# Three or four units per image sampled by matrix products beside an LSTM, in a four-stage image kernel on one core

## What is computed

```python
x = x + window_attention(gn(x))     # 8x8 query blocks, 14x14 keys, 4 heads of 8 channels
x = x + lstm(gn(x))                 # a sequence of 96 columns per image row, hidden size 128
x = x + deformable_conv(gn(x))      # 3x3, learned offsets and masks
x = x + block_transform(gn(x))      # M * block * M^T on 8x8 blocks
```

```python
x_off = g_lt * x[qx_lt, qy_lt] + g_rb * x[qx_rb, qy_rb] + g_lb * x[qx_lt, qy_rb] + g_rt * x[qx_rb, qy_lt]
x_off = x_off * m
out = conv2d(x_off, conv_w, stride=3)
```

## Time and profile before

| | us |
|---|---|
| median of 3 executions | 3617.43 |
| lowest, highest | 3611.35, 3619.76 |
| the profiled execution, its own time | 3624.01 |
| span of the profile, first to last instruction | 3622.2 |
| PE, DVE, POOL, ACT busy | 2785.3, 2479.2, 2380.0, 1263.4 |

### The profile page before, as it was taken

How to read it: one execution, slowest core, us unless ns; L and a number is a source line. 1 busy time by engine, 2 the same in 40 slices (tenths; PEclk the granted TensorE clock), 3 DMA queues, 4 the chain that set the end, 5 groups by cost and what they waited for, 6 DMA issues and landing times. The chain is left out here.

```text
span 3622.2 us, 59607 instructions
## 1 busy us (share of the span) xinstructions
PE 2785.3 (77%) x21833; PEld 2027.9 (56%) x21833; DVE 2479.2 (68%) x5480; ACT 1263.4 (35%) x3105; POOL 2380.0 (66%) x2445
## 2 busy tenths in 40 slices
PE   6979984885899748867998568668987376889882
PEld 4667763664676526646666346546665254555542
DVE  4754447985777669965777679756777675677763
ACT  4644433542433315523333145324333121222210
POOL 3200026777777777777777777777777777777774
PEclk9999996886899868876999779768999688999995
DMA  6622025764321346636212376543213432222211
GB/s 214 194 60 73 1 71 166 208 174 93 88 60 53 106 145 192 193 82 123 59 53 68 96 216 193 145 94 87 59 54 104 87 94 73 65 63 70 59 53 48
DMA packets 270803, 374.53 MB, mean 103 GB/s; under 512 B 109508, under 2 KB 181336, under 8 KB 269992
## 3 DMA queue, kind: packets, MB, share of 16 engines
q1 hardware_dynamic: 166688, 200.21, 19.2%
q0 software_dynamic: 76896, 157.64, 16.0%
q10 hardware_dynamic: 26928, 12.87, 1.6%
HBM read 270.08 MB, written 99.55 MB: 102 GB/s over the span
## 5 line engine op out<-in xcount | busy, mean ns | idle before, releaser
L769 POOL DMA_INDIRECT got<-sample_table,index x2403 | 2325.2, 968 | 1092.3 <-issue 726.6
L1618 PE MATMUL gates<-cells,row_hat 128*128 128x400 f32 x1782 | 653.3, 513 | 67.8 <-DVE spanned L1153 53.2
L1618 PEld LDWEIGHTS gates<-cells,row_hat 128*128 128x128 f32 x1782 | 332.7, 194 | 309.6 <-issue 84.2
L1175 DVE TENSOR_TENSOR got<-got,bank 128x864 f32<-128x864 f32 x267 | 279.6, 1047 | 242.5 <-DMA got<-sample_table,index 234.3
L852 ACT ACTIVATE pt<-gates 98x512 f32<-98x512 f32 x528 | 288.6, 594 | 325.8 <-PE gates L1726 304.7
L1826 PEld LDWEIGHTS gates<-hist,whh 128*128 128x128 f32 x2280 | 313.5, 205 | 138.7 <-DVE hist L1469 100.8
L1826 PE MATMUL gates<-hist,whh 128*128 128x96 f32 x2280 | 325.9, 290 | 53.8 <-DVE hist L1469 53.1
L1286 DVE TENSOR_REDUCE mx<-gates 128x2 f32<-128x392 f32 x576 | 295.5, 553 | 82.3 <-PE gates L1712 80.9
L1606 PE MATMUL bank<-turned,wout 128*128 128x96 f32 x1728 | 244.9, 304 | 131.5 <-DVE turned L1203 66.1
L1606 PEld LDWEIGHTS bank<-turned,wout 128*128 128x128 f32 x1728 | 239.0, 219 | 156.4 <-DVE turned L1203 110.5
L1712 PE MATMUL gates<-kst,qst 96*128 96x196 bf16 x1152 | 185.2, 278 | 119.7 <-DVE mx L1286 103.1
(11 more groups left out here) (188 smaller groups left out, 4791.6 us busy)
## 6 DMA issues: line engine op xcount, KB each, us to landing
kst<-k_parts SPq DMA_DIRECT2D x96, 441.0 KB
got<-sample_table,index POOLq DMA_INDIRECT x2403
qst<-q_parts SPq DMA_DIRECT2D x96, 288.0 KB
k_parts<-kp SPq DMA_DIRECT2D x24, 882.0 KB
k_parts<-kp SPq DMA_DIRECT2D x24, 588.0 KB
q_parts<-qp SPq DMA_DIRECT2D x24, 576.0 KB
spread<-locations ACTq DMA_DIRECT2D x84, 144.0 KB, 3.9
sample_table<-tab SPq DMA_DIRECT2D x12, 784.0 KB
```

Of the source, the lines that this page charges most:

```text
L769: pool.indirect_dma_start(out=got[:, g % RING, n, :], out_offset=None, in_=tables[p], in_offset=bass.IndirectOffsetOnAxis(ap=at, axis=0)). ...
L1175: dve.tensor_tensor(corners, corners, w[:, :, 0:3].unsqueeze(3).to_broadcast([P, NTAP, 3, C]), ALU.mult).then_inc(weighted, 1)
L1618: mm = pe.matmul(sums_of(s, h), row_hat[:, 3 * v % HATS + n // TAPS3, t, n % TAPS3, :], cells[:, t, C // 2 * h:C // 2 * (h + 1), :].rearra ...
```

## The change

Images 0 to 2 get four dense units each, 60 to 63, instead of three, 60 to 62; image 3 keeps its twelve. Gathered units are 264 instead of 267, dense units 24 instead of 21. The nine more taps lie in the same LSTM steps: 216 pieces from step 14 to 94 instead of 162. The due table gets a number for the first six points of an attention (BEGUN: units 7, 75, 147, which were about 2, 70, 140 in the even table), and the other numbers change: LSTMs are given 33, 34, 34 units (31, 31, 32 before), the end of preparation 3 has 214 due (210), transforms 0 and 1 one unit each (three each).

Cells of a unit, not of a group of three, are now the unit of transposition: 36 rows (9 taps by 4 cells) for each unit, up to four units in one bank, one copy by ACT per bank, and one store by SP for all units of an image. For image 3 all twelve units are transposed, copied and stored after its last positions; ACT waits there for one more thing, unit 207's transpose, since the copied rows now share their memory with dense samples. The dense samples have 4 slots (5 before). Groups in which units are left for gathering place their weights at the first of these.

```diff
-        stages += [(6 + 3 * NU, ATTENDED[p]), (W, STEPPED[p]), (prep_points(p), PREPARED[p])]
+        stages += [(6, BEGUN[p]), (3 * NU, ATTENDED[p]), (W, STEPPED[p]), (prep_points(p), PREPARED[p])]
...
-ATTENDED = (0, 28, 96, 167)
-STEPPED = (0, 59, 127, 199)
-PREPARED = (0, 68, 138, 210)
-SHARED = (213, 216, 230)
+BEGUN = (0, 7, 75, 147)
+ATTENDED = (0, 27, 97, 169)
+STEPPED = (0, 60, 131, 203)
+PREPARED = (0, 70, 142, 214)
+SHARED = (215, 216, 230)
...
-DENSE_GROUPS = tuple((p, 20) for p in range(LAST)) + ((LAST, 6), (LAST, 11), (LAST, 16), (LAST, 21))
+LUNITS = 4
+BATCHES = tuple((p, 60, LUNITS) for p in range(LAST)) + tuple((LAST, first, GUNITS) for first in (18, 33, 48, 63))
...
+USTEPS = LUNITS * NTAP
+LSTEPS = USTEPS * LAST
...
-SAMPLES = 2 * GUNITS - 1
-LOCATIONS = GUNITS * NTAP * CELLS
+SAMPLES = 4
+LOCATIONS = NTAP * CELLS
...
 def pieces_upto(t):
 
-    n = t - FIRST_PIECE + 1
-    return min(max(4 * (n // 2) + 3 * (n % 2), 0), PIECES * GSTEPS)
+    n, whole = max(t - FIRST_PIECE + 1, 0), W - 1 - FIRST_PIECE
+    return min(PIECES * USTEPS * (8 * (n // 2) + 5 * (n % 2)) // (4 * whole + 1), PIECES * USTEPS)
...
-    hats = [FIRST_HAT + NTAP * n + i for n in range(3 * GUNITS) for i in range(2 * KTILES)]
+    hats = [FIRST_HAT + (W - 1 - FIRST_PIECE) * n // (3 * LUNITS) + i for n in range(3 * LUNITS) for i in range(2 * KTILES)]
...
+        def banks_of(p):
+
+            return [(first, min(first + 4, IMAGE_UNITS[p])) for first in range(0, IMAGE_UNITS[p], 4)]
...
-                for i, d in enumerate(groups_of(p)):
-                    sp.wait_ge(rows_copied, d + 1)
-                    sp.dma_start(locations[d], located[:, i, :]).then_inc(rows_stored, 16)
+                sp.wait_ge(rows_copied, banks_upto(p + 1))
+                sp.dma_start(locations[p].rearrange("u r s -> r u s"),
+                             located[:, 0:P * IMAGE_UNITS[p]].rearrange("r (u s) -> r u s", s=P)).then_inc(rows_stored, 16)
...
-                for i, d in enumerate(groups_of(p)):
-                    act.wait_ge(rows_turned, d + 1)
-                    wait(act, dense_summed, GSTEPS * p)
-                    act.activation(located[:, i, :], located_ps[i], ACT.Copy).then_inc(rows_copied, 1)
+                wait(act, dense_summed, USTEPS * p)
+                for i, (first, last) in enumerate(banks_of(p)):
+                    act.wait_ge(rows_turned, banks_upto(p) + i + 1)
+                    if P * last > C * FINE:
+                        act.wait_ge(samp_turned, DENSE_UNIT[LUNITS * p - 1] + 1)
+                    act.activation(located[:, P * first:P * last], located_ps[i][:, 0:P * (last - first)], ACT.Copy).then_inc(rows_copied, 1)
...
-                if uu % GUNITS == 0:
+                if uu in PLACING:
+                    at -= uu % GUNITS
...
-                for i, d in enumerate(groups_of(p)):
-                    pe.wait_ge(dense_ready, d + 1)
-                    pe.transpose(located_ps[i], cell_rows[:, i].rearrange("p u n a -> p (u n a)"),
-                                 ident[:, :]).then_inc(rows_turned, 1)
+                pe.wait_ge(dense_ready, groups_of(p)[-1] + 1)
+                for i, (first, last) in enumerate(banks_of(p)):
+                    for u in range(first, last):
+                        mm = pe.transpose(located_ps[i][:, P * (u - first):P * (u - first + 1)], cell_rows[:, u].rearrange("p n a -> p (n a)"),
+                                          ident[:, :])
+                    mm.then_inc(rows_turned, 1)
```

More of the change, by code:

```diff
@@ L228, in dense_points @@
     steps, done, last = [LSTEPS] * len(due), LSTEPS, -1
-    for k in (k for p, k in DENSE_GROUPS if p == LAST):
-        usable = [i for i in points if i > last and due[i - 1] < PARTS * (UNITS * LAST + GUNITS * k + 1)]
+    for first in (first for p, first, _ in BATCHES if p == LAST):
+        usable = [i for i in points if i > last and due[i - 1] < PARTS * (UNITS * LAST + first + 1)]
         for m, i in enumerate(usable):
@@ L355, in network @@
             mx1 = sb("mx1", [P, CH, NTAP], where=a2)
[L356 to L359, removed]
+            cell_of = sb("cell", [P, LUNITS, NTAP], where=a2)
+            other_of = sb("other", [P, LUNITS, NTAP], where=a2)
+            inner_of = sb("inner", [P, LUNITS, NTAP], where=a2)
+            cell_rows = sb("cell_rows", [P, max(IMAGE_UNITS), NTAP, CELLS], where=a2)
         with ExitStack() as a3:
@@ L546, in hats_of @@
         def hats_of(d):
-            late = d - LAST
-            return first_hat if late <= 0 else later_hat[:, late - 1]
+            n = BATCHES[d][2]
+            return first_hat[:, 0:n] if d <= LAST else later_hat[:, d - LAST - 1]
         def sums_of(s, h):
@@ L555, in groups_of, with banks_upto @@
         def groups_of(p):
-            return [d for d, (of, _) in enumerate(DENSE_GROUPS) if of == p]
+            return [d for d, (of, _, _) in enumerate(BATCHES) if of == p]
+        def banks_of(p):
+            return [(first, min(first + 4, IMAGE_UNITS[p])) for first in range(0, IMAGE_UNITS[p], 4)]
+        def banks_upto(p):
+            return sum(len(banks_of(of)) for of in range(p))
         block = ctx.enter_context(nc.Block())
@@ L921, in lstm @@
                 if p > 0:
-                    for v in range(GUNITS * (p - 1), GUNITS * (p - 1) + SPREADS):
+                    for v in range(LUNITS * (p - 1), LUNITS * (p - 1) + SPREADS):
                         load_spread(v)
@@ L1133, in dense_positions @@
                     then(dve.tensor_scalar(other[:, :, :], cell[:, :, :], float(a), FAR, ALU.not_equal, ALU.mult))
-                    then(dve.tensor_tensor(cell_rows[:, i, :, :, a], other[:, :, :], py, ALU.add))
+                    then(dve.tensor_tensor(cell_rows[:, i:i + N, :, a], other[:, :, :], py, ALU.add))
                 then(dve.scalar_tensor_tensor(out=inner[:, :, :], in0=cell[:, :, :], scalar=float(-CELL), in1=px, op0=ALU.mult, op1=ALU.add))
                 hat = hats_of(d).rearrange("p u n f -> p (u n) f")
-                then(dve.tensor_tensor(hat, ccols[:, :].unsqueeze(1).to_broadcast([P, GUNITS * NTAP, FINE]),
-                                       inner[:, :, :].rearrange("p u n -> p (u n)").unsqueeze(2).to_broadcast([P, GUNITS * NTAP, FINE]),
+                then(dve.tensor_tensor(hat, ccols[:, :].unsqueeze(1).to_broadcast([P, N * NTAP, FINE]),
+                                       inner[:, :, :].rearrange("p u n -> p (u n)").unsqueeze(2).to_broadcast([P, N * NTAP, FINE]),
                                        ALU.subtract))
@@ L1547, in pixel_math @@
                 for d in groups_of(p):
-                    if first <= GUNITS * DENSE_GROUPS[d][1] < first + N:
+                    if first <= BATCHES[d][1] < first + N:
                         dense_positions(d)
@@ L1938, in prepare @@
                 combine()
-                wait(pe, dense_read, 2 * GSTEPS * p)
+                wait(pe, dense_read, 2 * USTEPS * p)
                 for i in range(EARLY):
```

68 lines of the change are left out of this document (37 added, 31 removed).

## The result

The changed kernel takes **3735.4 us** (3730.3 to 3748.7), the kernel before on the same chip 3614.6 us: a ratio of **1.034 [1.031, 1.037]**. It is 121 us slower, where 29 us faster was forecast, and lies outside the range. The profiled execution has a span of 3734.8 us, 112.6 us above the 3622.2 of before.

The account below looks back on a forecast made before the run. POOL's nearly unbroken gathers were taken as the bound. Removed gathers (33.7 us) and unit 211 starting at 2954 instead of 2949.3 us, with E unmoved, gave a 29 us gain: 3588 us, range 3571 to 3623.

Parts of the forecast that it names:

- The gathers' 33.7 us: POOL: 27 gathers fewer at 1.25 us each take 33.7 us off its time.
- The tail: Transforms 0 and 1 onward: unit 211 starts 72.7 us after E, with 54 units to go.
- E: Moment when DVE leaves image 3's preparation and starts transform 0's statistics: 2881 us before, forecast about 2881 after.
- Units moved to an attention's first points: First six attention points, 7, 5, 5 units for 2, 2, 2: counted at 0, may give or cost 10 us per attention.
- LSTM lengthened: LSTMs of images 1 to 3: each grows by 30 us (22 to 39, outer bound 43.5), +90 us in all.
- the waits for gathers: DVE, images 1 to 3: all 89.5 us of waits go, 17 us (0 to 35) come back.
- 14 us for the units: Attentions of images 1 to 3: four gathered units fewer at 3.4 us of DVE each, -14 us.
- The +4 us for the located units: Preparations: positions for 36 columns instead of 27, four transposes and a wider copy per image, about +4 us over three images.
- PE cannot hide any of it: Rival, LSTMs: added pieces delay the hidden state by their full length, 43.5 us per LSTM, 3628 us; chance 0.15.
- PE has room: Rival, LSTMs: they grow by 10 us or less, POOL stays the bound, full gain of 42 us, 3575 us; chance 0.17.
- No change: Rival: late rows for image 3 and costlier early attention points cut the gain to 7 us or less, about 3614; chance 0.12.

Follow-up runs that it names:

- the early read: The changed kernel with DVE reading each PSUM half in the LSTM step in which PE fills it, not the next: 3613.3 us, 0.9986 to the kernel before.
- the run with the doubled products: The kernel before with the first product of each half in the LSTMs run twice, 108 matmuls more per LSTM, in the old rhythm: 3675.9 us.

## Why the prediction was wrong

**Right.** The counts: 2376 gathers and 2592 dense matmuls. The gathers' 33.7 us (33.5 less busy time). The tail: the way from E to unit 211, 72.7 us forecast, is 71.3 after and 71.9 with the early read, and the gain of the span is 2910 - E to within 3 us in both. Units moved to an attention's first points cost nothing; they gained nothing either. The added products by themselves: +26, +26, +23 in the run with the doubled products, +34, +27, +24 with the early read, against 30.

**The failed step** is "LSTM lengthened". It asked only how much of 42 us PE could hide while it waits for the hidden state, and said of DVE's steps "PE is late anyway, so I count nothing". It did not ask what the new rhythm does to the order between PE and DVE: each piece waits until its PSUM half has been read, and the change makes a tap 2.25 steps long instead of 3, so that half of the refills fall into the step of the read. What the runs put in its place: +24 to 34 us of work and about **+40 us that come with PE standing behind DVE** (31 to 32 of them on rows of waits), in each LSTM (403.6, 405.1, 406.6 with the refills, 364.8, 362.3, 362.4 without). Its place can be read off the diff and the tables of steps. No LSTM of before shows the wait, since none has such a refill; but its page shows the same wait outside the LSTMs, 53.2 us at image 3's dense products, and the forecast neither used that line nor gave the wait a bound.

**The second step that failed** weighs less: the waits for gathers were taken off E in full, 72.5 of 89.5 us, and 14 us for the units. The waits went, all of them, though the forecast's reason, the longer LSTM, is only part of the cause: by itself it took away 25 us in the run with doubled products, and the table's larger LSTM shares had to be there too. But in the attentions 71.2 us of these waits (17.2, 23.0 and 31.0) and four units gave only 54 us, where the forecast had some 86 for all waits and units. Part of the freed time came back as DVE's wait for PE ahead of the row maxima, 27 us more; from 550 to 2950 us, before and after:

```profile
DVE mx L1286 <- PE gates L1712: 40.6, 30, 4.7
...
DVE mx L1307 <- PE gates L1733: 67.6, 45, 4.2
```

This step alone would have cost the forecast nearly all of its gain: with the early read the LSTMs grew by 28 us on average, as forecast, and still E comes at 2912.3 instead of 2881 and the kernel is 0.1% faster than before, not 0.8%. The +4 us for the located units rests on no row, and no run shows it: the preparations together came to -6.5 us for the -3 forecast.

**The rivals.** "PE cannot hide any of it" had the right sign, but neither the mechanism nor the size: its 43.5 us gives 3628; the LSTMs took 70, and PE's own added work was partly hidden all the same. "PE has room" fell the other way: 42 us of matmul cost 25. The Trainium skill, Perfetto Trace Analysis, Identifying the Most-Contended Engine, tells to judge PE's headroom by its share of the peak arithmetic rate (MFU) and by the weight loads' busy share, and not by matmul busy time. By the loads alone, 69%, there would have been room for it, and the run with doubled products speaks against that here. "No change" has nothing for it.

The range was too narrow: its upper end, 3623, stands for LSTMs longer by some 42 us, less than PE's own work with nothing hidden (43.5), and it left no room for a new wait. The prediction's own test was the right one: wrong if an LSTM grows by over 40.

## What to carry to other kernels

When a schedule written out by hand gets more work in the same steps, count for every single-buffered tile whether its refill now falls into the step in which it is read; this takes two tables and no profile, and here it decided about 40 of 70 us per LSTM. A wait that the old trace shows in one stage, here 53.2 us outside the LSTMs, is a hint to look for it in the stage that gets the work. An in-order engine that waits there holds up all that is queued behind it, here the recurrence. And a lead gained in one stage is worth only as much as the ring behind it can hold: time beyond six slots came out as waits at the full ring until more units were due in the longer stage.

## What was not expected of the hardware

Of work added to an engine that was 91% busy by the trace, a good part was still hidden: 108 matmuls (42 us) more made each LSTM 23 to 26 us longer, so 16 to 19 us were hidden, about the 17.0 us for which weight loads had waited for the hidden state. Busy share gave neither bound; the waits of the loads came close. The forecast had used these waits as its bound on what can be hidden. That is an observation of three LSTMs, and no run tests it further.
